# Two-layer transformer kernel: tokens kept in the residual buffer, second Hadamard products at the group that uses them, W2's DMAs issued by ScalarE

## The reference, cut to what matters

```
xn = layernorm(x)                                   # no weights
x  = x + attn0(xn) + ffn0(xn)
attn0(n):  # a rank-8 state-space layer and a rank-8 feed-forward
    h = scan(layernorm(n) @ W_in + b_in);  y = n + h @ W_out + b_out + layernorm(n) * D_skip
    return y + relu(layernorm(y) @ W_down + b_down) @ W_up + b_up
ffn0(n):   hidden = fwht(silu(n @ W1.T) * (n @ W3.T));  return hidden @ W2.T   # 2048 wide
```

## Time and profile before

| | |
|---|---|
| median of 3 runs | 1873.22 us (1871.0 to 1873.24) |
| the profiled execution's own time | 1869.85 us |
| its span in the trace | 1868.1 us |
| TensorE busy | 1723.7 us, 92% of the span |
| VectorE, ScalarE, GpSimd busy | 56%, 39%, 14% |
| mean granted clock of TensorE | 0.971 |

### The profile page before, as it was taken

The page is one execution under the profiler, slowest core; times in us unless marked ns, Lnnn a source line. Parts: engine busy times, 40 slices in busy tenths (PEclk is TensorE's granted clock), DMA queues, the critical chain, the costliest instruction groups (busy, mean ns, idle before and its releaser), DMA issues. The chain is left out here.

```text
span 1868.1 us, 24728 instructions
## 1 busy us (share of the span) xinstructions
PE 1723.7 (92%) x8364; PEld 1381.7 (74%) x8364; DVE 1042.1 (56%) x1788; ACT 735.8 (39%) x1530; POOL 265.9 (14%) x224
## 2 busy tenths in 40 slices
PE   6899999999999769979999899958899999999997
PEld 4566877777788658867777777747678888888885
DVE  4221365454522443449999799956365647556554
ACT  4521211221111332239999899953221222212121
POOL 3000210310310021100000000018203203203200
PEclk9999999999999979989999999979899999999999
DMA  9830110110100017833444444335200001101011
GB/s 302 282 103 1 57 46 18 51 46 6 51 6 35 34 68 239 305 157 86 126 124 133 126 123 126 96 135 179 90 1 34 25 11 34 34 0 34 11 45 45
DMA packets 87689, 159.78 MB, mean 86 GB/s; under 512 B 8345, under 2 KB 39449, under 8 KB 85922
## 3 DMA queue, kind: packets, MB, share of 16 engines
q1 hardware_dynamic: 87586, 158.52, 26.7%
HBM read 105.01 MB, written 53.48 MB: 85 GB/s over the span
## 5 line engine op out<-in xcount | busy, mean ns | idle before, releaser
L1784 DVE TENSOR_TENSOR pt_lo<-p_turn,pt_hi 128x512 fp32r<-128x512 f32 (+3 forms) x384 | 201.2, 551 | 24.9 <-ACT pt_hi L1759 17.4
L1777 DVE TENSOR_REDUCE row_top<-p_score 128x1 f32<-128x128 f32 (+7 forms) x256 | 189.8, 751 | 21.1 <-PE p_score L1711 20.9
L1229 DVE TENSOR_TENSOR hid<-hid,p_up 128x512 f32<-128x512 f32 x64 | 44.0, 688 | 277.9 <-PE p_up L737 259.4
L1751 ACT ACTIVATE prob<-p_score,row_top 128x128 f32<-128x128 f32 (+7 forms) x256 | 189.6, 744 | 8.0 <-DVE row_top L1777 5.9
L1722 PE MATMUL p_turn<-ident,prob 128*128 128x128 f32 x1152 | 183.2, 278 | 3.9 <-DVE pt_lo L1784 3.6
L1759 ACT ACTIVATE pt_hi<-p_turn 128x512 fp32r<-128x512 f32 (+3 forms) x384 | 182.0, 493 | 12.0 <-PE p_turn L1722 8.2
L1737 PE MATMUL p_o<-pt_hi,v 128*128 128x512 f32 (+3 forms) x384 | 149.2, 396 | 3.8 <-ACT o_both L1767 3.1
L1722 PEld LDWEIGHTS p_turn<-ident,prob 128*128 128x128 f32 x1152 | 133.4, 143 | 17.7 <-DVE pt_lo L1784 4.4
L990 ACT ACTIVATE hid<-p_gate 128x512 f32<-128x512 f32 x64 | 38.2, 598 | 268.3 <-PE p_gate L737 268.3
L1709 PE MATMUL p_score<-stack 128*128 128x512 f32 (+3 forms) x384 | 129.6, 392 | 14.0 <-PEq L53 7.0
L294 DVE TENSOR_TENSOR ff_hid<-ff_hid,ff_p_up 128x512 f32<-128x512 f32 x64 | 43.9, 686 | 162.8 <-PE ff_p_up L183 160.9
(11 more groups left out here) (242 smaller groups left out, 3955.4 us busy)
## 6 DMA issues: line engine op xcount, KB each, us to landing
stack<-qk_parked SPq DMA_DIRECT2D x256, 128.0 KB, 3.7
qk_parked<-qk SPq DMA_DIRECT2D x16, 1024.0 KB, 3.9
raw<-in_wgu SPq DMA_DIRECT2D x32, 256.0 KB
v_parked<-v_out SPq DMA_DIRECT2D x16, 512.0 KB, 4.8
v<-v_parked SPq DMA_DIRECT2D x8, 1024.0 KB, 8.9
o_parked<-o_both SPq DMA_DIRECT2D x64, 128.0 KB
o<-o_parked SPq DMA_DIRECT2D x8, 1024.0 KB, 9.0
ff_raw_gu<-in_wgu SPq DMA_DIRECT2D x16, 512.0 KB, 3.7
```

What stands on the lines that cost most here:

```text
L1751: act.activation(prob[r // QB][:, h % 2, r % QB, 0:width_of(r)], p_score[:, r % 2, 0:width_of(r)], ACT.Exp, bias=top[:, r:r + 1], accum_ou ...
L1777: dve.tensor_reduce(top[:, r:r + 1], p_score[:, r % 2, 0:width_of(r)], AX_X, ALU.max, negate=True).then_inc(topped, 1)
L1784: dve.tensor_tensor(pt_lo[:, slot, c0:W], p_turn[:, (BL * h + j) % TB, c0:W], pt_hi[:, slot, c0:W].bitcast(F32), ALU.subtract).then_inc(sp ...
```

## The change

Tokens: ACT's `norm_first` writes the normalized tokens to four buffers `n1[q]`, which lie where the hidden values' second buffer, `h_hi`'s second half, `d_hi` and `d_lo` will be; `res` keeps x. `store_n1` and `reload_x` are gone. `load_tok` reads x, and ACT normalizes each token tile anew (`tok_norm`, 16 of 128x512). The scales stay in `inv1` and `neg1`.

W2: slices are now four of 16 chunks, all 512 columns, in runs of 8 KB. The 16 first products (`rotate(s, h)`) stand at the start and in unit 0. A half is stored once; the store writes runs of 2 KB. The second products are `turn_down(g, c)`, one for each of the 16 chunks: they read a raw chunk from the ring, ahead of halves (1, 0), (1, 1), (2, 0) and (2, 1) of unit 4 g + 1. ACT's `down_round` makes `d_hi` and DVE's `down_rest` makes `d_lo` straight from PSUM. `store_slice` and GpSimd's `split_d` are gone.

Queues: ACT issues `turn_w`, the four slices and the four stores. SP waits for all four stores before it loads raw 8.

Order: the third quarter is turned ahead of unit 0's last chunk and the fourth ahead of unit 1's first (before: units 1 and 2). On ACT `norm_first(2)` and `norm_first(3)` follow in unit 0 at c = 1 and c = 2.

```diff
         def halves_before(u, c, j):
+            n = 2 * c + j + 1
+            return [divmod(n, 2)] if u == 0 and 2 <= n < 2 * SL else []
+        def downs_before(u, c, j):
+            return [(u // TT, 2 * c - 2 + j)] if u % TT == 1 and c in (1, 2) else []
...
+            for s in range(SL):
+                sp.wait_ge(half_out[s], 16)
             for k in range(8, 8 + RING):
                 load_raw(k)
...
+            def turn_down(g, c):
+                k = d_item(g, c)
+                landed(pe, k)
+                if c >= 2:
+                    pe.wait_ge(d_split, NC * g + c - 1)
+                elif g:
+                    pe.wait_ge(added, J * (TT * g - 1) + c + 3)
+                else:
+                    pe.wait_ge(rot_copied, NCH)
+                pe.matmul(p_out[:, c % 2], turn_w[:, 1], raw[:, k % RING], start=True, stop=True).then_inc(d_turned, 1)
...
+            def load_slice(s):
+                act.dma_start(rot[s][:], w2c[:, SR * s:SR * s + SR]).then_inc(slice_in[s], 16)
+            def store_half(s):
+                act.wait_ge(rot_copied, SR * s + SR)
+                act.dma_start(halves[:, SR * s:SR * s + SR], rot[s][:]).then_inc(half_out[s], 16)
...
+            def rot_copy(s, h):
                 for i in range(2):
                     m = 2 * h + i
+                    act.wait_ge(rot_done, SR * s + m + 1)
+                    act.activation(rot[s][:, m], p_out[:, i], ACT.Copy).then_inc(rot_copied, 1)
+                if h:
+                    store_half(s)
+            def down_round(g, c):
+                act.wait_ge(d_turned, NC * g + c + 1)
+                if g == 0:
+                    act.wait_ge(turned, 3 * KD)
+                act.activation(d_hi[:, c], p_out[:, c % 2], ACT.Copy, scale=ROOT).then_inc(d_round, 1)
...
                     if u == 0 and c == 1:
                         x_round_quarter(1, 0)
                         root(3, slice(2 * Q, 4 * Q))
+                        norm_first(2)
                     if u == 0 and c == 2:
-                        norm(2, 0)
-                    if u == 0 and c == 3:
-                        norm(3, 0)
-                    if u == 1 and c == 0:
+                        norm_first(3)
                         x_round_quarter(2, 0)
+                    if inside and not odd and c >= 2:
+                        tok_norm(Q * q + c - 2)
...
+            def down_rest(g, c):
+                dve.wait_ge(d_round, NC * g + c + 1)
+                if g == 0:
+                    dve.wait_ge(turned, 4 * KD)
+                dve.scalar_tensor_tensor(d_lo[:, c], p_out[:, c % 2], ROOT, d_hi[:, c].bitcast(F32), ALU.mult,
+                                         ALU.subtract).then_inc(d_split, 1)
...
                         if c == 1:
                             rsqrt(5 + q, quarter(q), mean3)
                             feed(q)
                         if c == 3:
                             stack_hf_rest(q)
-                    for turn_of in turns_before(u, c, 0) + turns_before(u, c, 1):
-                        if turn_of[0] == 2 and turn_of[2] == 0:
-                            first_rest(turn_of[1])
+                    for down in downs_before(u, c, 0) + downs_before(u, c, 1):
+                        down_rest(*down)
```

More of the change, by code:

```diff
@@ L333, in up, with layer_zero @@
         return self.sem
[L336 removed]
+def layer_zero(nc, t, ident, x_hi, x_lo, spare, half_turned, parked):
     R = 8
@@ L568, in _ @@
             load_tok(1)
-            for k in range(8 + RING, 19):
+            for k in range(12 + RING, 23):
                 load_raw(k)
@@ L572, in _ @@
                 load_tok(i)
-            for k in range(19, 23):
+            for k in range(23, 27):
                 load_raw(k)
@@ L576, in _ @@
                 load_tok(i)
-            for k in range(23, 31):
+            for k in range(27, 35):
                 load_raw(k)
@@ L580, in _ @@
                 load_tok(i)
-            for k in range(31, 35):
+            for k in range(35, 39):
                 load_raw(k)
@@ L584, in _ @@
                 load_tok(i)
-            for k in range(35, 44):
+            for k in range(39, 48):
                 load_raw(k)
@@ L909, in root, with norm_first, norm_last @@
                 act.activation(sd[:, a], var[:, a], ACT.Sqrt).then_inc(sd_done, 1)
-            def norm(q, last):
-                act.wait_ge(mean_neg, 3 + q + 1 if last else min(q, 2) + 1)
-                if last:
-                    act.wait_ge(res_out[q], 32)
+            def norm_first(q):
+                act.wait_ge(mean_neg, min(q, 2) + 1)
+                for j in range(Q):
+                    i = Q * q + j
+                    act.activation(n1[q][:, j], res[:, i], ACT.Identity, bias=neg1[:, i:i + 1],
+                                   scale=inv1[:, i:i + 1]).then_inc(n1_done, 1)
+            def norm_last(q):
+                act.wait_ge(mean_neg, 3 + q + 1)
+                act.wait_ge(res_out[q], 32)
                 for i in range(Q * q, Q * q + Q):
@@ L997, in quarter @@
                 return slice(Q * q, Q * q + Q)
+            act.dma_start(turn_w[:], t["turns"]).then_inc(turn_in, 16)
+            for s in range(SL):
+                load_slice(s)
             root(1, quarter(0))
-            norm(0, 0)
-            rot_copy(1, 0, 0)
-            rot_copy(1, 0, 1)
+            norm_first(0)
+            rot_copy(0, 0)
+            rot_copy(0, 1)
             x_round_quarter(0, 0)
             root(2, quarter(1))
-            norm(1, 0)
+            norm_first(1)
             for u in range(UNITS):
@@ L1052, in _ @@
                 hi(u, NC - 1)
+                if inside and not odd:
+                    tok_norm(Q * q + 2)
+                    tok_norm(Q * q + 3)
                 if u == UNITS - 2:
                     root(9, quarter(0))
-                    norm(0, 1)
+                    norm_last(0)
                 if u == UNITS - 1:
@@ L1253, in _ @@
             add_eps(quarter(0))
-            rsqrt(1, quarter(0), mean_neg)
+            rsqrt(1, quarter(0), mean_neg, inv1, neg1)
             x_rest(0, 0)
@@ L1257, in _ @@
             add_eps(quarter(1))
-            rsqrt(2, quarter(1), mean_neg)
+            rsqrt(2, quarter(1), mean_neg, inv1, neg1)
             for u in range(UNITS):
```

236 lines of the change are left out of this document (86 added, 150 removed).

## The result

The changed kernel takes 1891.84 us (median of 4 runs, 1889.94 to 1892.93), the kernel before 1872.96 us (4 runs, 1871.0 to 1873.24): a ratio of 1.0102 with a 95% interval of 1.0084 to 1.0119, 1.0% slower. The forecast was +10.4 us and 1883.6 us; it came to +18.9 us. The range, 1873 to 1893 us, held it; the likeliest case's own, 1879 to 1888 us, did not. The profiled execution took 1892.93 us with a span of 1891.2 us, 23.1 us above the span before. Of these, 19.6 us are there when the last output of layer zero is added to `res` (667.4 us before, 687.0 us after).

The account below looks back on a forecast made before the run. The prediction took TensorE's instruction stream, with holes in it, as the bound. Savings of 13.85 us against additions of 4.2, 13.1, 3.4 and 3.5 us gave +10.4 us on 1873.2, so 1883.6 us, range 1873 to 1893.

Parts of the forecast that it names:

- the likeliest case: The forecast itself, whole kernel: +10.4 us, 1883.6 us, chance 0.48, own range 1879 to 1888 us.
- (a): After each slice's first second product, TensorE's four waits for DVE's d_lo go: 7.1 us saved.
- (b): TensorE's wait at 62.19 us, behind norm(3) on ACT, goes: 2.05 us saved.
- (c): TensorE's "issue" waits where a reloaded half was due go with the reloads: 1.3 us saved.
- (d): Clock dips near 62 and 106 us go with the waits there, 1.7 us each: 3.4 us saved.
- (e): norm_first(2) ahead of ACT's copies lengthens TensorE's wait at rotate(3, 0), near 49 us: 4.2 us added.
- (f): In units 1, 5, 9, 13 turn_down(g, 2) waits for DVE's down_rest, 2.15 or 4.4 us each: 13.1 us added.
- (g): Two clock dips of 1.7 us behind TensorE's new holes: 3.4 us added, ends 0 and 6.8.
- (h): At the start, ACT's slice loads delay x by 3.0 us and a store adds 0.5: 3.5 us added.
- one slice between the halves: At the start, turn_w and one slice of 2.7 us get between x's halves: +3.0 us.
- The rival of the start shared row by row: At the start, queues alternate by rows, 2 KB against 8 KB: 8.7 us instead of 3.5, 1888.8 us; chance 0.2.
- rests are absorbed: At turn_down(g, 2), DVE reaches down_rest before TensorE comes, so new holes and dips vanish: -6.2 us, 1867.0 us; chance 0.12.

Follow-up runs that it names:

- experiment 1: Changed kernel with down_rest moved ahead of product(u, c), or right behind lo, on VectorE: 1871.94 us, ratio 0.9997 to the kernel before.
- experiment 12: Changed kernel with tok_norm cut to column 0 of 512, the other 511 left raw: 1889.34 us, one run.
- experiments 10 and 11: Changed kernel with slices 1 to 3 issued behind root(1): 1892.09 us; that kernel with GpSimd's splits held behind the first norm's small operations: 1891.92 us.
- experiment 4: Changed kernel with turn_w and the four slices issued by SyncE, behind x's first and second quarters: 1887.36 us, ratio 1.0078 to the kernel before.

## Why the prediction was right in sign and too small

- **(a), (b), (c)**: 7.1, 2.05 and 1.3 us of waits are gone. Right.
- **(d)**, 3.4 us: half right. The dip near 106 us went; the one near 60 us stayed (0.86 and 0.79), since the wait of (e) took the place of the old one. The prediction counted that dip as saved although it put a longer wait beside it.
- **(e)**, 4.2 us: right, 6.98 against 2.79 us.
- **(f)**, 13.1 us: right, 12.9 us; experiment 1 takes exactly these waits away.
- **(g)**, 3.4 us: the step that failed. It priced a hole of 4.4 us as one of 2.15 us, and only every second one. In the steps of units 4, 8 and 12 the growth is 12.1 + 10.6 + 7.6 = 30.3 us; less the products, 12 x 0.91 = 10.9 us, and the three waits, 10.8 us, 8.6 us are left for a lower clock. Experiment 1 puts 1.7 to 2.7 us behind each of the three waits, 7 in all. The rest, 1.6 us, stays when the waits are gone: it is the dip behind the old wait for `state_stack` in unit 5, and unit 7's, the growth of 1.5 us there, is another. The kernel before has both waits without the dips. The prediction looked for dips only behind the new holes; why these come is open. That unit 1's wait brought none fits its "about half of the cases".
- **(h)**, 3.0 + 0.5 us: the mechanism was right, the size was not. x came 5.3 us later, and the first wide product 1.7 us beyond that, 7.0 in all: the second pair of first products now stands behind the norm, ahead of the transposes, at the lower rate shown above. Neither "one slice between the halves" nor "equal bytes" (2.1 us) nor strict rows (8.2 us): up to 11 us the slices moved 2.3 MB to x's 1.0, or two packets to three. The store of the first half took 0.39 us ahead of `x_hi` (0.5 costed).
- **Costed at nothing**: the products' place (12 out, 12 in), `tok_norm` (experiment 12) and half 3, whose store took 4.4 us where TensorE then didn't wait for raw: right. Units 3 and 4 kept their length (41.7 us and 36.2 after 36.3 between first adds): right. Unit 2 did not, 43.8 us after 45.6: the fourth quarter's 16 transposes left it for unit 1, which the prediction had named but not carried into its list of signs.

Up to unit 3 the terms make -13.85 - 10.3 + 4.2 + 2.15 + 1.7 + 3.5 = -12.6 us, and -12.0 were measured, though (h) alone is 3.5 us over; some 3 us of small gains, which no run here takes apart, cover it. From there to unit 15 they make 10.3 + 10.95 + 1.7 = 23 us, and 31.6 were measured: products 10.9, waits 10.8, lower clock behind these waits 7.0, and two dips behind old waits, about 3. This is the whole of the miss up to the end of layer zero. That the total stayed within the range owes something to luck: (g) and (h) were both too small, and some 3 us of gains that nobody forecast stood against them.

The rival of the start shared row by row named the right thing to doubt (8 KB rows against 2 KB) and came nearest the total, 1888.8 us, but for a reason that gives only 2.3 us of its 5.2. The rival "rests are absorbed" had the mechanism by which the change becomes harmless: experiment 1 makes it true by an edit. It gave 1867.0 us; the measured 1871.9 us has the start's excess and the dips that stayed in it.

The Trainium skill (DMA: Bandwidth & Descriptors, section Queues, rings and completion order) has an engine take turns between queues packet by packet; the queue views of the first two kernels agree as far as they go, 0.66 and 0.69 packets to one with rows of 8 and of 2 KB, and the third, 0.46, doesn't repeat it. Some two slices and not one got between; what the trace counts as a packet carried 6.5 KB on average, less than one row. On experiments 10 and 11 the Trainium skill (SBUF — State Buffer, section SBUF: two separate sides) says that VectorE and GpSimd share one pair of ports under an exclusive lock and that the later one waits for the whole instruction, which the equal ends above bear out. By its words that needs VectorE to have two SBUF inputs beside a GpSimd operation that reads SBUF, or to be in a 2-port mode. The long operations on `z_t`, `inv` and `neg` have two inputs, and the reciprocal, with one, was not held up. `z_var` has one and was; its mode no trace shows.

## What to carry to other kernels

Before an instruction is put where TensorE wants its result at once, look at what stands ahead of it on the engine that makes the result; here a few lines moved up were worth 19.9 us in the new kernel and 9.0 us in the old (1872.41 us in the same series), more than the redesign. Price a new hole by its length and by the matmuls behind it: 2.15 us of waiting cost 3.9 in unit 12's step and no more than its own length in unit 1, and 4.3 us cost 7. And expect dips to move: with the same old waits of 2.17 us in them, the kernels here had between none and four. What the first compute waits for belongs on the queue ahead of everything else, in as few issues as can be; a second queue beside it takes its share from it, the larger the longer its rows.

## What the runs showed of the hardware

- Two queues side by side moved about two packets to three in two kernels, with 6.5 and with 1.7 KB in a packet of the second queue (0.46 to one in a third kernel, with slices of 32 partitions). With rows of 8 KB against x's 2 KB, x's 1 MB landed at 11.56 us, with rows of 2 KB at 7.83, with slice 0 behind it on its own queue at 6.20 us.
- Around a wait of 4.32 us TensorE's clock stood at 1.2 GHz from 252 to 258 us, although it worked all the time from 253.53 us on. In the trace of experiment 4 the same wait was followed by only two slow wide matmuls (0.63 and 0.52 us).
- The same wait of 2.17 us, four times in each kernel, was followed by a dip of the clock in all four places, in two or in none.
- An operation of 128x4 on VectorE, 0.16 us alone, with two inputs, took up to 1.12 us beside GpSimd's split of 128x512, and ended with it.
- Beside x, transfers of 1 MB into 128 partitions moved at 26 GB/s an engine and transfers of 256 KB into 32 partitions at 15, both worked out from the queue views.
- Making the first wide product earlier by 2.4 us gave 0.6 us, since the clock was low just then.
